# A recurrent mixer and a quantized feed-forward layer: the prologue in another order

## What is computed

```python
x = L0_attn_hidden_states                       # (2, 512, 512), f32
xn = _layernorm(x)
proj = xn @ in_proj_w.T                         # gate 8192 | x 8192, B 8*128, C 8*128 | dt 128 heads
xBC = silu(conv4(xBC) + conv_b)                 # depthwise, 4 taps along the sequence
x, Bm, Cm = split(xBC)
dt = clip(softplus(dt + dt_bias), 0.001, 100)   # A = -(1..128), chunks of 128
Y = chunked scan: (C B^T * decay) (x dt)  +  C state exp(cs)  +  x D
yg = Y * silu(gate)
s = (yg * rsqrt(mean over each group of yg^2 + eps)) * norm_w @ out_proj_w.T
g = silu(W2 (silu(W1 xn) * (W3 xn)))            # W1, W2, W3: 4-bit values times scales
out = x + s * g
```

## Time and profile before

| | us |
|---|---|
| median of 3 runs (lowest, highest) | 1844.73 (1844.5, 1845.83) |
| the profiled execution | 1846.68 |
| its span on the core | 1844.9 |
| TensorE busy | 1785.9 (97%) |
| VectorE busy | 1420.4 (77%) |
| GpSimd busy | 1271.1 (69%) |
| ScalarE busy | 1239.1 (67%) |
| DMA | 203.35 MB, mean 110 GB/s |

### The profile page before, as it was taken

The page is one execution under the profiler, slowest core; times in us unless marked ns, Lnnn a source line. Parts: engine busy times, 40 slices in busy tenths (PEclk is TensorE's granted clock), DMA queues, the critical chain, the costliest instruction groups (busy, mean ns, idle before and its releaser), DMA issues.

```text
span 1844.9 us, 30182 instructions
## 1 busy us (share of the span) xinstructions
PE 1785.9 (97%) x10292; PEld 1460.9 (79%) x10292; DVE 1420.4 (77%) x2188; ACT 1239.1 (67%) x2463; POOL 1271.1 (69%) x874
## 2 busy tenths in 40 slices
PE   4799999999999999999999999999999999989998
PEld 4588888888888888888888888888888888877777
DVE  5768887887887878878888887887878878858840
ACT  4786768777777677776777677667777776633320
POOL 2478777776876787767776786777777777656641
PEclk8999999999999999999999999999999999999999
DMA  3433333332423333233323342333333332235422
GB/s 134 155 125 104 106 99 129 103 106 94 135 98 99 106 120 107 93 117 104 125 91 118 103 129 93 111 99 116 112 104 98 118 118 97 85 91 154 133 85 93
DMA packets 122466, 203.35 MB, mean 110 GB/s; under 512 B 22800, under 2 KB 60048, under 8 KB 122064
## 3 DMA queue, kind: packets, MB, share of 16 engines
q1 hardware_dynamic: 120592, 197.71, 33.6%
q10 hardware_dynamic: 1728, 3.78, 0.5%
HBM read 194.09 MB, written 7.34 MB: 109 GB/s over the span
## 4 chain that ended last, share of the span: by engine, by line
PE 76%; POOL 7%; issue 5%; DVE 4%; ACT 4%; DMA 1%; SPq 0%; POOLq 0%; ACTq 0%; DVEq 0%
PE bank L130 13%; PE bank L132 13%; PE bank L131 12%; PE bank L467 10%; PE bank L505 6%; PE bank L549 5%; PE bank L551 5%; PE bank L550 5%; PE bank L589 3%; PE bank L685 3%; POOL yt L1236 2%; POOL yt L1240 2%; ACT L752 1%; DVE ec L1000 1%; POOL up_lo L1283 1%
## 5 line engine op out<-in xcount | busy, mean ns | idle before, releaser
L1236 POOL TENSOR_TENSOR yt<-yt,ec 128x384 f32<-128x384 f32 x128 | 175.5, 1371 | 365.7 <-DVE ec L1000 365.6
L954 DVE SCALAR_TENSOR_TENSOR z<-bank,cw_all,z 128x511 f32<-128x511 f32 (+2 forms) x480 | 358.3, 747 | 18.3 <-ACT z L709 5.0
L745 ACT ACTIVATE lm<-lm,hp 128x128 f32<-128x128 f32 x1024 | 313.2, 390 | 1.2 <-ACT stage L870 0.4
L991 DVE TENSOR_TENSOR xdt<-bank,hp 128x512 f32<-128x512 f32 x128 | 88.3, 690 | 238.3 <-PE bank L589 237.1
L966 DVE SCALAR_TENSOR_TENSOR lm<-lm,gm 128x1024 f32<-128x1024 f32 x128 | 261.5, 2043 | 12.0 <-ACT lm L745 12.0
L130 PE MATMUL bank<-xn_hi,conv_hi 128*128 128x512 f32 x640 | 262.6, 410 | 6.0 <-DVE z L954 4.9
L1245 POOL TENSOR_TENSOR conv_lo<-raw_x,conv_hi 128x512 fp32r<-128x512 f32 x128 | 228.2, 1783 | 34.7 <-ACT conv_hi L699 34.7
L132 PE MATMUL bank<-xn_hi,conv_lo 128*128 128x512 f32 x640 | 252.0, 394 | 0.0
L131 PE MATMUL bank<-xn_lo,conv_hi 128*128 128x512 f32 x640 | 250.8, 392 | 0.0
L1240 POOL TENSOR_TENSOR yt<-yt,gate 128x512 f32<-128x512 f32 x128 | 226.7, 1771 | 18.4
L130 PE MATMUL bank<-xn_hi,gate_hi 128*128 128x512 f32 x512 | 212.5, 415 | 0.0
(11 more groups left out here) (128 smaller groups left out, 3978.9 us busy)
## 6 DMA issues: line engine op xcount, KB each, us to landing
lm<-cs_d SPq DMA_DIRECT2D x128, 512.0 KB, 3.9
raw_x<-w_conv_dram SPq DMA_DIRECT2D x128, 256.0 KB, 3.0
ec<-e_d SPq DMA_DIRECT2D x256, 96.0 KB, 3.6
raw_g<-w_gate_dram SPq DMA_DIRECT2D x64, 256.0 KB, 2.8
raw_o<-w_out_dram SPq DMA_DIRECT2D x64, 256.0 KB, 2.7
raw_b<-w_conv_dram SPq DMA_DIRECT2D x32, 256.0 KB, 3.4
q_raw<-w1q_dram SPq DMA_DIRECT2D x10, 256.0 KB, 3.2
q_s<-w1s_dram SPq DMA_DIRECT2D x10, 256.0 KB, 3.5
```

The source lines that it names most:

```text
L745: e = act.activation(lm[m % 3][:, u, :], lm[m % 3][:, u, :], ACT.Exp, bias=hp[bd.seq][:, Q_CS, k1, u:u + 1])
L954: dve.scalar_tensor_tensor(z[:, zi, d:SEQ], src[:, 0:SEQ - d], cw_all[:, bd.group, pos, 3 - d:4 - d], z[:, zi, d:SEQ], ALU.mult, ALU.add). ...
```

## The change

1. SyncE: the loads of x's tiles 0 and 1 of group 0 go out ahead of the second sequence's x tiles; the steps leave them out.
2. VectorE: all four moments of the second sequence come after `low_xn(0)`; before, two stood ahead of `norm(0)`.
3. TensorE: after the second sequence's tiles are turned it projects x's tile 0, C, then `turn_q(0)`, x's tile 1, `steps_dt(1)`, gate tile 0, the scores. Before it was `steps_dt(1)`, C, x's tile 0, `turn_q(0)`, x's tile 1, gate tile 0, the scores.
4. ScalarE: the calls of the FILL steps are taken apart and put in the order below. x's tile 0 is evicted ahead of `round_xn(1)`, `softplus(1)` comes after `first_hp` and x's tile 1, `stage_hp(0)` moves from step 1 of body 0 to the prologue, ahead of the Silus of x, B and C. `stage_hp(1)` moves from the head of step 2 to step 1, between `weights` and `work_b`.
5. C's first projection goes to `xt[:, 3]` in place of `z[:, 2]`, so it needs no wait for B's Silu; both Silus come together at step 6.
6. VectorE: the taps of B, `weigh(0)`, the taps of x's tile 0, then `low_xn(1)`, the taps of C, step 6, and only then the second sequence's part.
7. `turn_q(1)` one step earlier.
8. In the drain: one feed-forward projection, `up(0, 0, P, 1, 1)`, goes ahead of the last body's sums of squares.
9. Line 1188: tensor_tensor becomes scalar_tensor_tensor with a factor of 1.0.

```diff
@@ SyncE
-                if bx.exists():
+                if bx.exists() and (bx.n, kx) not in ((0, 0), (0, 1)):
@@
             step(FILL, 1)
+            for i in range(2):
+                sp.dma_start(raw_x[:, i, :], w_conv[0, X_POS[i]]).then_inc(rawx_in[i], 16)
             for t in range(NC, TT):
@@ TensorE
             steps_dt(0, ps_a)
-            step(FILL, 3)
+            extra(FILL, 3)
             for t in range(NC, TT):
                 turn(t)
...
-            steps_dt(1, ps_y)
-            step(FILL, 4)
-            step(FILL, 5)
-            pe.wait_ge(xnlo_done, TT)
-            pe.wait_ge(pd, N_CUM + 2)
-            turn_q(0)
-            step(FILL, 6)
+            conv(FILL, 5)
+            extra(FILL, 4)
+            pe.wait_ge(xnlo_done, TT)
+            pe.wait_ge(pd, N_CUM + 1)
+            turn_q(0)
+            conv(FILL, 6)
+            steps_dt(1, ps_y)
+            gate_mm(FILL, 6)
+            extra(FILL, 6)
             step(FILL, 7)
@@
-                if k == 2:
+                if k == 1:
                     pe.wait_ge(pd, 2 * (N_CUM + 2))
                     pe.wait_ge(qt_ev, NQ)
                     turn_q(1)
@@ TensorE, drain
                     ss = sums(before)
+                    if not body.exists():
+                        pe.wait_ge(t0_done, TILES * BODIES)
+                        up(0, 0, P, 1, 1, 0)
...
-            up(0, 0, P, 1, 0)
-            pe.wait_ge(t0_done, TILES * BODIES)
-            up(0, 0, P, 1, 1)
+            up(0, 0, P, 1, 0, 0)
@@ ScalarE
             round_xn(0)
-            step(FILL, 2)
+            round_bc(FILL, 2)
+            round_gate(FILL, 2)
             softplus(0, ps_a)
-            weights(FILL, 3)
-            weights(FILL, 4)
+            round_x(FILL, 4)
+            raw_bc(FILL, 4)
+            round_bc(FILL, 4)
+            round_gate(FILL, 3)
+            decays(0)
+            work_b(FILL, 5)
             round_xn(1)
-            decays(0)
+            raw_bc(FILL, 5)
+            round_gate(FILL, 4)
+            first_hp()
+            round_x(FILL, 5)
+            work_b_x(FILL, 6)
+            round_gate(FILL, 5)
             softplus(1, ps_y)
-            work_b(FILL, 4)
-            step(FILL, 5)
-            first_hp()
-            step(FILL, 6)
+            round_x(FILL, 6)
+            round_gate(FILL, 6)
+            stage_hp(0)
+            work_b(FILL, 6, False)
             step(FILL, 7)
             decays(1)
 
-            def begin(k):
-                if k in (1, 2):
-                    stage_hp(k - 1)
+            def step(body, k):
+                work_a(body, k)
+                weights(body, k)
+                if body.n == 0 and k == 1:
+                    stage_hp(1)
+                work_b(body, k)
@@ ScalarE, B and C
+            return xt[:, 3, :] if body.n == 0 and i == 1 else z[:, 2, :]
...
+                    if k == 6 and nx.is_number(0):
+                        silu_bc(nx, 0)
+                        silu_bc(nx, 1)
@@ VectorE
             combine(0)
-            moments(range(NC, NC + 2))
             norm(0)
...
-            moments(range(NC + 2, TT))
+            moments(range(NC, TT))
...
             cumulate(0)
+            taps(Body(0, 0, 0), BC_POS[0], z_bc(Body(0, 0, 0), 0), ps_g, tap0_b, taps_b, 0)
+            weigh(0)
+            taps(Body(0, 0, 0), X_POS[0], z[:, 0, :], ps_a, tap0_x, taps_x, 0)
             low_xn(1)
...
-            step(FILL, 2)
-            step(FILL, 4)
-            weigh(0)
+            dve.wait_ge(dc_done, 2)
+            taps(Body(0, 0, 0), BC_POS[1], z_bc(Body(0, 0, 0), 1), ps_g, tap0_b, taps_b, 1)
+            step(FILL, 6)
             relu_dt(1, ps_y)
-            step(FILL, 5)
             cumulate(1)
-            step(FILL, 6)
             step(FILL, 7)
             weigh(1)
@@
-                    dve.tensor_tensor(cols[1], cols[0], cols[1], ALU.mult).then_inc(val_done[i], 1)
+                    dve.scalar_tensor_tensor(cols[1], cols[0], 1.0, cols[1], ALU.mult, ALU.mult
+                                             ).then_inc(val_done[i], 1)
```

More of the change, by code:

```diff
@@ L476, in project_bc, with y_off @@
                     for q in range(KT)]).then_inc(bp_done, 1)
-            def step(body, k):
+            def y_off(body, k):
                 n = TILES * body.n + k
-                nx = body.plus(1)
                 pv, kp = at(body, k, -1)
@@ L487, in step, with conv @@
                                 range(1, NC)).then_inc(yo_done, 1)
+            def conv(body, k):
                 bd, kx = at(body, k, 3)
@@ L514, in step, with gate_mm @@
                                 ).then_inc(st_mm, 1)
+            def gate_mm(body, k):
+                nx = body.plus(1)
                 bd, kg = at(body, k, 2)
@@ L552, in step, with extra @@
                     mm.then_inc(o_done, 1)
+            def extra(body, k):
+                nx = body.plus(1)
                 before = body.plus(-1)
@@ L590, in step @@
                     mm.then_inc(tx_done, 1)
+            def step(body, k):
+                y_off(body, k)
+                conv(body, k)
+                y_diag(body, k)
+                gate_mm(body, k)
+                out_mm(body, k)
+                extra(body, k)
+                turn_x(body, k)
             def turn(t):
@@ L641, in up @@
                     for kk in range(KT)])
-                if i == 1:
+                if i == last:
                     mm.then_inc(up_done, 1)
@@ L690, in _, with round_x @@
         def _(act):
-            def weights(body, k):
+            def round_x(body, k):
                 bd, kx = at(body, k, 4)
@@ L734, in weights @@
                     act.activation(wout_hi[pos // 4][:, pos % 4, :], raw_o[:, :], ACT.Copy).then_inc(whi_o, 1)
+            def weights(body, k):
+                round_x(body, k)
+                raw_bc(body, k)
+                round_bc(body, k)
+                round_gate(body, k)
+                round_out(body, k)
             def work_a(body, k):
@@ L766, in gate_raw, with silu_bc, work_b_x @@
                     act.activation(gate[:, kg % 4, :], ps_g[:, :], ACT.Copy).then_inc(gev_done, 1)
-            def work_b(body, k):
-                n = TILES * body.n + k
-                nx = body.plus(1)
+            def silu_bc(nx, i):
+                act.wait_ge(taps_b, 3 * (2 * nx.n + i) + 3)
+                if i == 0:
+                    wait(act, bt_mm, nx.n)
+                else:
+                    wait(act, yo_done, TILES * (nx.n - 1))
+                act.activation(b_t[:, :] if i == 0 else c_t[:, nx.seq, :], z_bc(nx, i), ACT.Silu
+                               ).then_inc(bs_done, 1)
+            def work_b_x(body, k):
                 bd, kx = at(body, k, 3)
@@ L778, in work_b @@
                                    bias=cw_all[:, bd.group, pos, 4:5]).then_inc(tap0_x, 1)
+            def work_b(body, k, with_x=True):
+                n = TILES * body.n + k
+                nx = body.plus(1)
+                if with_x:
+                    work_b_x(body, k)
                 pv, kp = at(body, k, -1)
@@ L807, in work_b @@
                     gate_raw(body, k)
[L808 to L815, removed]
-                                       ).then_inc(bs_done, 1)
+                    if k in (4, 6) and nx.exists() and not nx.is_number(0):
+                        silu_bc(nx, k // 2 - 2)
+                    if k == 6 and nx.is_number(0):
+                        silu_bc(nx, 0)
+                        silu_bc(nx, 1)
                     bd, kx = at(body, k, 3)
@@ L920, in ahead @@
                     unpack(0, 0, P, UP[s - 5:s - 4])
-            over_bodies(act, step, ahead, begin)
+            over_bodies(act, step, ahead)
             unpack(1, 1, P, UP)
@@ L946, in _, with taps @@
         def _(dve):
-            def taps(bd, pos, zi, src, ready, done, i):
+            def taps(bd, pos, dst, src, ready, done, i):
                 dve.wait_ge(ready, i + 1)
@@ L1069, in step @@
                 if bd.exists():
-                    taps(bd, X_POS[kx], kx % 2, ps_a, tap0_x, taps_x, TILES * bd.n + kx)
+                    taps(bd, X_POS[kx], z[:, kx % 2, :], ps_a, tap0_x, taps_x, TILES * bd.n + kx)
                 if crowded:
```

30 lines of the change are left out of this document (19 added, 11 removed).

## The result

The changed kernel takes **1849.45 us** (median of 10 executions, 1847.39 to 1851.65), the kernel before, run beside it, 1845.03 (1843.93 to 1846.89): a ratio of 1.0022, 95% interval 1.0012 to 1.0031, so about 4.1 us slower. Measured again (the tenth experiment) it took 1849.38 against 1845.40, ratio 1.0026, interval 1.0016 to 1.0036. The forecast was 1847.4 in a range of 1841.0 to 1852.5: inside it, 2 us over the forecast. By the prediction's own limit (up to 1848.4 counts as the same) it is slower, which had a chance of 0.35 against 0.54 for the same: the time was met within the range, the outcome with the largest chance was not. The change is 0.2% of the time.

A forecast was written before the change was run, and what follows sets the result against it. TensorE, busy 97% of the span, was taken as the bound, so only its idle and half-clock time could be won. +4.1 +2.3 -2.1 -1.6 = +2.7 us on the 1844.73 median gave 1847.4, range 1841.0 to 1852.5.

The forecast's parts named there:

- D2: Start of body 0's third diagonal product (line 512 after, 505 before), a milestone; 100.87 us in the kernel before.
- Part 1: Layer norm in the prologue: norm(0) 1.3 us sooner, B's projection no earlier, early loads hidden; worth nothing.
- part 7: Line 1188's multiplication as scalar_tensor_tensor: same rate, 0 us, at most +1.5.
- part 2: Prologue, x's first tile: early load and rounding, low part behind gate tile 1's on GpSimd; projection starts at 31.6 us.
- the rival: Line 1188 at half rate in VectorE's feed-forward loop: +16 us on top of +2.7, 1863 us; chance 0.05.
- Part 3: Prologue: round_xn(1) and low_xn(1) queue behind x's eviction and taps; new 3.0 us pause before turn_q(0).
- Part 4: From steps_dt(1) to the scores: ScalarE's 12.1 us queue delays scores by 4.1 us; half clock adds 2.3.
- Part 5: Body 0: the old 4.01 us pause goes, a 4.5 us wait for x's taps replaces it; -2.1 us.
- Part 6: Drain: a feed-forward projection fills a 3.04 us TensorE wait, last out products run at full clock; -1.6 us.
- fast path: Rival: prologue pauses of 2 to 3 us leave the clock up, c_t ends near 61.4; 1843.2 us, chance 0.20.
- clearly faster case: Rival: a wait between x's first tile and the scores doesn't bind, body 0 starts as before; 1839.7 us, chance 0.11.
- slow path: Rival: half clock in x's first tile, turn_q and x's second tile, c_t at 68; 1850.7 us, chance 0.18.

The follow-up runs named there:

- experiment 10: The changed kernel again with no edit, beside the kernel before: 1849.38 us against 1845.40, ratio 1.0026.
- experiment 1: Kernel before with only the drain edit, one feed-forward projection ahead of the last body's sums of squares: 1843.37 us against 1844.85, ratio 0.9995.
- experiment 2: Kernel before with only the line 1188 multiplication as scalar_tensor_tensor: 1844.29 us, ratio 1.0001.
- experiment 7: Kernel before with only stage_hp(0) moved from step 1 of body 0 to behind first_hp in the prologue: 1838.40 us, ratio 0.9963.
- experiment 8: Kernel before with stage_hp(0) moved to behind first_hp, plus the drain edit: 1838.08 us, ratio 0.9958.
- experiment 9: Kernel before with only the moments edit, all four of the second sequence behind low_xn(0): 1844.79 us against 1845.40, ratio 1.0001.
- experiment 11: Changed kernel with stage_hp(0), stage_hp(1) and round_xn(1)/low_xn(1) moved, and the old drain restored: 1838.55 us, ratio 0.9963 to the kernel before.
- experiment 3: Changed kernel with stage_hp(0) moved up on ScalarE behind the rounding of x's tile 1: 1845.27 us, ratio 1.0003 to the kernel before.
- experiment 4: Changed kernel with stage_hp(1) back at the head of step 2 of body 0: 1843.82 us, ratio 0.9997 to the kernel before.

## Why the prediction was right, and where it was off

The starts of the changed kernel, forecast and measured. The forecast ones were counted on the trace of before, whose norm(0) began at 12.72; in the four other traces of the same prologue (experiments 1, 2, 7 and 8) it began at 11.6 to 11.8, about 1 us earlier, so about 1 us of lead is no effect of the change:

| | forecast | trace of after | experiment 10 |
|---|---|---|---|
| B | 22.4 | 21.36 | 21.57 |
| x's first tile | 31.6 | 29.78 | 30.65 |
| turn_q(0): start, us | 40.2, 3.4 | 39.76, 1.97 | 39.29, 3.61 |
| scores | 65.3 | 63.34 | 64.53 |
| pause for x's taps in body 0 | 4.5 | 4.72 | 4.73 |
| D2 | 105.2 (100.87 + 4.3) | 103.81 | 105.04 |
| pause behind the last out products | 5 | 4.93 | 4.94 |

**Parts 1 and 7, nothing.** Right in the time. Experiment 2 measured the multiplication by itself, experiment 9 the moments; the early loads were only seen in the trace to delay nothing. Part 1 had no word of the half clock that the longer pause ahead of B can bring (0.72 in experiments 9 and 10, 1.00 in the trace of after, from 21 to 27 us); part 2 had it. On the rule of the Trainium skill weighed there ("Vector Engine (DVE) Microarchitecture Reference", Points that are easy to get wrong), by which the form with two sources outside bf16 runs at half rate: read as half the rate of tensor_tensor, as the rival had it, the trace doesn't agree. With an int32 and an f32 source the form has a median of 0.693 us, mostly for 512 elements, as tensor_tensor has. (The upper end given for part 7, 33 times 0.05, is 1.65 and not 1.5.)

**Part 2, x's first tile.** The order of the queues was right. The prediction had TensorE turning tiles until about 31; it had ended by then and waited 2.34 to 3.26 us for x's low part. Both of the part's cases occurred. In the trace of after B is fast and x runs partly at the lower level, behind the longer pause. In experiment 10 B runs partly at half clock, x starts 0.9 us later and runs at full clock. turn_q(0) came at nearly the same time (39.76 and 39.29).

**Part 3, the new wait.** Right in place and size: 2.61 and 2.90 us for 3.0. Whether half clock follows is not fixed, 1.97 us in one execution and 3.61 in the other. Undoing it gave 4.4 us by the ratios, uncertain by 2, and 3.0 from x to the end of the transposes in the traces.

**Part 4, ScalarE's chain ahead of the scores.** Right. By sum it had 12.1 us from softplus(1)'s start to c_t's end; the trace of after has 11.9 (51.30 to 63.20). The scores are late by 4.1 in the mean of executions: 61.26, 58.39, 58.74 and 61.13 in the four traces with the old order (before, experiments 1, 2 and 9), mean 59.9, and 63.34 and 64.53 with the new, mean 63.9. Half clock behind them: from the scores to B's transposes 7.4 us before (61.26 to 68.61) and 9.9 after (63.34 to 73.23), +2.5 for +2.3.

**Part 5, body 0: the step that was mis-sized.** The new pause was right (4.72 and 1.6 of clock; undone, 5.0 us). The old pause that it replaces was not. I took it at its 4.01 us with half clock behind it, as the one trace had it, and counted -2.1 for the exchange. From B's transposes to D2 that trace has 32.3 us and so has experiment 2; but the old order in experiment 1 has 29.4, because there the half clock fell ahead of the wait and was absorbed. Experiment 9 is of the same kind: 36.8 us from the scores to D2 as in experiment 1, against 39.6 in the other two. The changed kernel has 30.6 both times. So the exchange gains 1.7 us in two executions of the old order and loses 1.2 in the other two: about **-0.3 where I had -2.1**, from four traces and two.

**Part 6, the drain.** Right in its mechanism: the out products at full clock, the accumulation 1.5 us nearer to the sums, the new pause of 4.93 with slack behind it. 2.0 us for 1.6, and in two of the five traces with the old drain the clock is down already for the sums, which take 1.55 and 1.62 us (experiments 9 and 11) in place of 1.02.

**The sum.** +4.1 +2.5 -0.3 is +6.3 at D2 (the means: 98.1 with the old order, 104.4 with the new), less 2.0 is +4.3; the medians say +4.1 and +4.8 by the ratios. The forecast of +2.7 lacks that 1.8 of part 5, part of it made good by the drain. The base holds the same mistake: the profiled execution of before was 2 us over the median, and the forecast took those 2 us off the changed kernel's time as well. At D2 that trace is 2.8 us later than the mean of the four with the old order. Half of it lies ahead of the scores (61.26 against 59.9), where the changed kernel too was 1.4 us earlier than counted on that trace (63.9 against 65.3), so this half was rightly taken off. The other half lies between B's transposes and D2 (32.3 against 30.9): it is the old pause with its half clock, which the change replaces. Part 5 had counted it as a gain already, so it was counted twice.

**The rivals.** The fast path (1843.2) needed pauses of 2 to 3 us to leave the clock up. Some did, but not all in one execution, and the scores came at 63.3 and 64.5. The clearly faster case needed a wait that doesn't bind; all did. The slow path's 1850.7 lies nearer to the medians than the forecast, but its mechanism, c_t at 68 us, was in neither trace. The likelier outcome was missed by the size of one term: 0.54 stood on "the same" because the forecast lay 2.7 us over a base with 3.7 allowed, and a sum 1.6 us larger lies outside it. That the measured time fell within a range 11.5 us wide owes something to that width.

## What to carry to other kernels

When TensorE is the bound, look for blocks on other engines that nobody waits for soon (a staging copy, a store) and that stand in a queue ahead of something TensorE waits for. Here their places were worth 4 to 7 us each, while no run shows what the new order of TensorE's own work is worth: `stage_hp(0)` moved by itself gave 6.8 us in the old order, and three such blocks made the new order 10 us faster than the old instead of 4 slower. Price a pause together with the clock behind it, and before you credit a change with a pause that it removes, see whether that pause has the same length in a second execution. A stretch that is the same in all traces (here 1549.1 to 1549.4 us) turns single profiled executions into a measurement of what lies ahead of it.

## What the runs showed of the hardware

The same instructions spread over some 6 us from one execution to the next (1841.36 to 1847.27 in 33 executions of the kernel before on one chip). In four traces of the old order D2 spreads over 5.7 us (95.19 to 100.87). Of that 2.8 us are where TensorE's lower clock falls in body 0 (36.8 or 39.6 us from the scores to D2); the rest lies ahead of the scores, and about 1 us of it is norm(0)'s start. After pauses of 2.54 (experiment 3), 2.61 (after), 2.89 (experiment 4) and 2.90 us (experiment 10) the same sixteen transposes took 1.97, 1.97, 2.69 and 3.61 us; the lower clock can come ahead of a wait, which absorbs some of it, or behind it. What decides between the two isn't settled here. The Trainium skill ("TensorE: Matmul & The Clock Gate", Part 1: The HAM clock gate) says of the rise at a kernel's start that what the chip watches runs free of that start, so that one kernel sees its clock change at different places from run to run. The traces of experiments 1 and 2 agree with that in the outcome, in mid-kernel; no run here tests the mechanism.
